# A graph network's attention stage: scores interleaved two source blocks at a time, and one mask product fewer

## What is computed

```python
q = x @ Wq + bq
k = x @ Wk + bk
v = x @ Wv + bv
logits = jnp.sum(q[dst] * k[src], axis=-1) * scale
m = jax.ops.segment_max(logits, dst, num_segments=n)
ex = jnp.exp(logits - m[dst])
denom = jax.ops.segment_sum(ex, dst, num_segments=n)
alpha = ex / denom[dst]
agg = jax.ops.segment_sum(alpha[:, None] * v[src], dst, num_segments=n)
out = agg + x @ Ws + bs
return jax.nn.elu(out)
```

## Time and profile before

| | |
|---|---|
| time, median of 3 runs | 849.43 us (847.42 to 849.62) |
| the profiled execution: its time, its span | 856.0 us, 854.2 us |
| PE busy, share of the span | 755.5 us, 88% |
| PE weight loads | 655.8 us, 77% |
| DVE | 740.0 us, 87% |
| ACT | 505.8 us, 59% |
| POOL | 263.3 us, 31% |
| mean granted TensorE clock | 0.983 of full speed |

### The profile page before, as it was taken

How to read it: one execution, slowest core, us unless ns; L and a number is a source line. 1 busy time by engine, 2 the same in 40 slices (tenths; PEclk the granted TensorE clock), 3 DMA queues, 4 the chain that set the end, 5 groups by cost and what they waited for, 6 DMA issues and landing times.

```text
span 854.2 us, 22930 instructions
## 1 busy us (share of the span) xinstructions
PE 755.5 (88%) x8801; PEld 655.8 (77%) x8848; DVE 740.0 (87%) x888; ACT 505.8 (59%) x1013; POOL 263.3 (31%) x205
## 2 busy tenths in 40 slices
PE   0258999999999999999999687899999999999996
PEld 0146777777777777777775466799999999999996
DVE  6776799999999999999994537899999999999982
ACT  4859766767677667676775251445456455445534
POOL 4634000000000000000000320556766766766766
PEclk9999999999999999999999798899999999999998
DMA  9821112313213123122131612203433433432400
GB/s 252 264 78 79 79 79 105 125 77 135 95 77 153 77 95 135 77 125 105 77 153 79 254 56 77 77 13 149 160 105 134 160 123 116 160 137 105 157 7 11
DMA packets 17661, 96.63 MB, mean 113 GB/s; under 512 B 2610, under 2 KB 8860, under 8 KB 11100
## 3 DMA queue, kind: packets, MB, share of 16 engines
q1 hardware_dynamic: 14572, 90.02, 27.8%
q0 software_dynamic: 3056, 6.17, 2.6%
HBM read 51.55 MB, written 44.63 MB: 113 GB/s over the span
## 4 chain that ended last, share of the span: by engine, by line
PE 70%; DVE 12%; issue 10%; ACT 5%; another core or an unknown queue 1%; DMA 1%; DVEq 1%; POOL 0%; POOLq 0%; ACTq 0%; PEldq 0%; PEld 0%
PE bank L1278 17%; PE bank L1288 16%; PE bank L1117 14%; PE bank L1107 5%; PE bank L1146 5%; DVE oh_key L901 5%; PE bank L1144 5%; DVE kT L838 3%; PE bank L1275 2%; PE bank L1241 2%; ACT kT L543 1%; PE bank L1246 1%; PE bank L1084 1%; DVE mx L1029 1%
## 5 line engine op out<-in xcount | busy, mean ns | idle before, releaser
L481 POOL TENSOR_TENSOR sm<-sm,mbc 128x896 f32<-128x896 f32 (+1 forms) x100 | 186.2, 1892 | 77.5 <-ACT mbc L703 77.5
L1117 PE MATMUL bank<-wsb,hvb 128*128 128x512 f32 (+1 forms) x350 | 165.2, 578 | 13.7 <-DVE kT L838 12.4
L1278 PE MATMUL bank<-qT,kT 128*128 (+1 forms) x1250 | 168.0, 279 | 6.9 <-issue 4.3
L1144 PE MATMUL bank<-oh_key,oh_lo 128*128 128x100 bf16 x1600 | 170.4, 208 | 1.9 <-ACT wst L607 1.9
L1146 PE MATMUL bank<-oh_key,oh_lo 128*128 128x50 bf16 x3200 | 170.8, 187 | 0.0
L1278 PEld LDWEIGHTS bank<-qT,kT 128*128 128x128 f32 x1250 | 163.8, 196 | 5.0 <-DVEq L178 1.2
L1146 PEld LDWEIGHTS bank<-oh_key,oh_lo 128*128 128x128 bf16 x3200 | 163.7, 97 | 1.1
L1144 PEld LDWEIGHTS bank<-oh_key,oh_lo 128*128 128x128 bf16 x1600 | 155.8, 97 | 7.7 <-issue 5.5
L589 ACT COPY wsb<-bank 128x512 f32<-128x512 f32 (+1 forms) x175 | 88.0, 552 | 106.4 <-PE bank L1107 106.4
L1288 PE MATMUL bank<-vals,sm 128*128 128x129 f32 x1250 | 148.5, 276 | 0.0
L1029 DVE TENSOR_REDUCE mx<-sm 128x128 f32<-128x3200 f32 x25 | 146.2, 5846 | 0.9
(11 more groups left out here) (123 smaller groups left out, 697.9 us busy)
## 6 DMA issues: line engine op xcount, KB each, us to landing
gt<-gst SPq DMA_DIRECT2D x25, 1600.0 KB, 5.6
gl_sb<-gt SPq DMA_DIRECT2D x25, 1600.0 KB, 6.7
records<-rec SPq DMA_DIRECT2D x1, 2015.0 KB
out<-res SPq DMA_DIRECT2D x24, 64.0 KB, 1.6
src_i<-in_src SPq DMA_DIRECT2D x1, 403.0 KB, 6.5
w_in<-in_edge_weight SPq DMA_DIRECT2D x1, 403.0 KB, 6.9
dst_i<-in_dst SPq DMA_DIRECT2D x1, 403.0 KB, 7.4
dstn_i<-in_dst_next SPq DMA_DIRECT2D x1, 403.0 KB, 7.3
```

Source lines behind the costliest of these rows:

```text
L481: pool.tensor_tensor(part, part, mbc[:, v % 2:v % 2 + 1, :].to_broadcast([P, n, P]), ALU.subtract).then_inc(sub_done, 1)
L1117: T.matmul(ps(6 + at)[:, 0:n], hvb[:, w, :], wsb[:, at, 0:n], start=True, stop=True).then_inc(l0_mm, 1)
L1144: T.matmul(cells, lo, oh_key[:, u, m, 0:2 * KEYS, i], start=True, stop=False, skip_group_check=True)
L1278: ins = T.matmul(score_bank(g)[:, j * P:(j + 1) * P], kT[:, (a + j) * P:(a + j + 1) * P], qT[:, bass.ds(t * P, P)], start=g < LIFT, stop=T ...
```

## The change

The groups become 6, 6, 6 and 8 blocks, which makes room for 26 (`NTP`): `sm` and `gl_sb` get a 26th block. It is set up once: its part of `gl_sb` to a large negative number by POOL, its place in the last group's PSUM bank to zero by DVE. `sm` is laid out in pairs of blocks, with the two values of one destination side by side (`twos`), so `mask` writes every other word of a pair's 256, the maximum reads two words side by side and then hops to the next pair, and the weights of a values product are 128 words 8 bytes apart. `LIFT` becomes 2: PE does no mask product for group 1, ACT's `absent` starts at group 2, and DVE lifts group 1 too.

```diff
-SG = [(0, 7), (7, 6), (13, 6), (19, 6)]
+SG = [(0, 6), (6, 6), (12, 6), (18, 8)]
+NTP = NT + 1
-LIFT = 1
+LIFT = 2
...
+        def twos(v, a, n):
+            return sm[:, v, a * P:(a + n) * P].rearrange("p (k d i) -> p k d i", d=P, i=2)
...
+            pool.memset(gl_sb[:, :, NT * P:NTP * P], -FLOOR).then_inc(pad_ready, 1)
...
-                    part = sm[:, v, a * P:(a + n) * P].rearrange("p (h d) -> p h d", d=P)
-                    pool.tensor_tensor(part, part, mbc[:, v % 2:v % 2 + 1, :].to_broadcast([P, n, P]),
-                                       ALU.subtract).then_inc(sub_done, 1)
+                    part = twos(v, a, n)
+                    top = mbc[:, v % 2, :].unsqueeze(1).unsqueeze(3).to_broadcast([P, n // 2, P, 2])
+                    pool.tensor_tensor(part, part, top, ALU.subtract).then_inc(sub_done, 1)
...
+            V.memset(score_bank(NSG - 1)[:, (NT - SG[-1][0]) * P:SG[-1][1] * P], 0.0).then_inc(pad_ready, 1)
...
-                V.tensor_tensor(sm[:, v, a * P:(a + n) * P], score_bank(g)[:, 0:n * P],
-                                gl_sb[:, v, a * P:(a + n) * P], ALU.add).then_inc(masked, 1)
+                V.tensor_tensor(twos(v, a, n).rearrange("p k d i -> p k i d"),
+                                score_bank(g)[:, 0:n * P].rearrange("p (k i d) -> p k i d", d=P, i=2),
+                                gl_sb[:, v, a * P:(a + n) * P].rearrange("p (k i d) -> p k i d", d=P, i=2),
+                                ALU.add).then_inc(masked, 1)
...
+                if live(t + 1):
+                    for g in range(1, LIFT):
+                        lift(t + 1, (v + 1) % RING, turn + (v + 1) // RING, g)
                 if now:
                     mask(t, v, 3)
                 if now:
                     dve.wait_ge(masked, 2 + (t + 1) * NSG)
-                    V.tensor_reduce(mx[:], sm[:, v, :].rearrange("p (h d) -> p d h", d=P), AX, ALU.max).then_inc(mx_ready, 1)
+                    V.tensor_reduce(mx[:], twos(v, 0, NTP).rearrange("p k d i -> p d k i"), AXY, ALU.max).then_inc(mx_ready, 1)
...
-                for h in range(a, a + n):
-                    ins = T.matmul(ps(4 + v % 2)[:, 0:D + 1], sm[:, v, h * P:(h + 1) * P], vals[:, h, :], start=h == 0,
+                for h in range(a, min(a + n, NT)):
+                    weights = twos(v, h - h % 2, 2).rearrange("p k d i -> p (k d) i")[:, :, h % 2]
+                    ins = T.matmul(ps(4 + v % 2)[:, 0:D + 1], weights, vals[:, h, :], start=h == 0,
```

More of the change, by code:

```diff
@@ L11 @@
 AX = mybir.AxisListType.X
+AXY = mybir.AxisListType.XY
 F32 = mybir.dt.float32
@@ L82 @@
 STEPS = NT + 3
-assert sum(n for _, n in SG) == NT and NSG % 2 == 0 and LOOP_TO < NT
+assert sum(n for _, n in SG) == NTP and all(n % 2 == 0 for _, n in SG) and NSG % 2 == 0 and LOOP_TO < NT
 TG = [(a, min(4, NT - a)) for a in range(0, NT, 4)]
@@ L287, in build_gnn @@
         res = sb(s4, "res", [P, 2, D])
-        sm = sb(s4, "sm", [P, RING, NT * P])
-        gl_sb = sb(s4, "gl_sb", [P, RING, NT * P])
+        sm = sb(s4, "sm", [P, RING, NTP * P])
+        gl_sb = sb(s4, "gl_sb", [P, RING, NTP * P])
         s4.close()
@@ L293, in build_gnn @@
         gl = [sem(f"gl{k}") for k in range(RING)]
-        absent_ready, lifted = sem("absent_ready"), sem("lifted")
+        absent_ready, lifted, pad_ready = sem("absent_ready"), sem("lifted"), sem("pad_ready")
         s_ready, masked, mx_ready, mt_ready, m_ready, dg_ready, mb_ready, mbc_ready = (
@@ L401, in load_g @@
                     sp.wait_ge(masked, 2 + (t - RING + 1) * NSG)
-                sp.dma_start(gl_sb[:, v, :], gt[bass.ds(tile, 1), :, :, :].rearrange("b p h n -> (b p) (h n)")).then_inc(gl[v], 16)
+                sp.dma_start(gl_sb[:, v, 0:NT * P], gt[bass.ds(tile, 1), :, :, :].rearrange("b p h n -> (b p) (h n)")).then_inc(gl[v], 16)
             for t in range(RING):
@@ L675, in mark_absent @@
                     act.wait_ge(s_ready, (t - 1) * NSG)
-                nc.scalar.activation(absent[:, v % 2, LIFTED:], gl_sb[:, v, LIFTED:], ACT.Relu, scale=-STEEP).then_inc(absent_ready, 1)
+                nc.scalar.activation(absent[:, v % 2, LIFTED:], gl_sb[:, v, LIFTED:NT * P], ACT.Relu, scale=-STEEP).then_inc(absent_ready, 1)
             root(0)
@@ L1028, in dve_step @@
                     dve.wait_ge(masked, 2 + (t + 1) * NSG)
-                    V.tensor_reduce(mx[:], sm[:, v, :].rearrange("p (h d) -> p d h", d=P), AX, ALU.max).then_inc(mx_ready, 1)
+                    V.tensor_reduce(mx[:], twos(v, 0, NTP).rearrange("p k d i -> p d k i"), AXY, ALU.max).then_inc(mx_ready, 1)
+            dve.wait_ge(pad_ready, 2)
             for g in range(LIFT):
@@ L1272, in scores @@
                 pe.wait_ge(masked, t * NSG + g + 1)
-                for b, e in ((0, 4), (4, n)):
+                for b, e in ((0, 4), (4, min(n, NT - a))):
                     if g >= LIFT:
```

## The result

The changed kernel takes 843.99 us, median of 12 runs, beside 849.27 us for the kernel before on the same chip: ratio 0.9941, 95% interval 0.9927 to 0.9954. That is 5.3 us faster, by the interval 3.9 to 6.2. I had forecast 837.5 (829 to 859), faster by 12, so the direction was right and the size less than half.

What follows compares the result with a forecast made beforehand. PE was taken to bound stage 4's step, with DVE close behind. Savings of 5.7 us over 21 steps, 5.5 at the start and 1.2 at the end, less 0.2 set-up, made 12.2: about 837.5 us, range 829 to 859.

Steps and rivals of the forecast that it cites:

- What bounds the kernel: Stage 4's step of 12.62 us: PE's own work 12.45 plus a 0.17 wait for mask 1; DVE occupied 12.02.
- either engine alone could gain almost nothing: Stage 4's step: work taken from only PE or only DVE leaves 12.62 us or little less.
- The maximum: DVE's maximum over blocks: 5.86 us falls to 3.5 with pairs; rival that pairs gain nothing, 867 us, chance 0.05.
- the masks' writes: DVE's masks writing every other word: no cost; rival of 0.78 ns an element, 867 us, chance 0.14.
- POOL: Subtraction on POOL: 7.45 us becomes 7.75, hidden; rival that POOL becomes the bound, 862 us, chance 0.05.
- PE's removed columns: PE's mask products: 640 columns fewer at 0.42 ns each, 0.267 us a step less.
- The weights 8 bytes apart: Values products' weight loads on PE: no cost taken; rival of 45 ns a load, 890 us or more, chance 0.03.
- the two ends that I kept, 0 and 45 ns: Cost range per strided weight load: none, from stage 2's line 1107, up to 45 ns, 2.3 us a step.
- DVE's occupied time: DVE in a stage 4 step: 12.02 us falls to 10.8, under PE's 12.35, idle 1.5 mostly ahead of mcol.
- The ends: Stage 4's first steps, where PE waits for the maximum: 5.5 us saved (4.0 to 7.3); its last: 1.2.
- Sums: Totals: 12.2 us saved, median 849.43 to about 837.5; chances given as faster 0.73, slower 0.22.

Runs made afterwards that it cites:

- e9: The changed kernel with DVE masking group 1 right behind group 0, ahead of the lift and mcol; ratio to the kernel before 0.9885, step 12.50 us.
- e10: The changed kernel with LIFT = 3 and DVE masking group 1 right behind group 0; ratio to the kernel before 0.9803, step 12.18 us.
- e4: The kernel before with only LIFT = 2, the second lift ahead of mask 3; ratio to the kernel before 0.9927, step 12.43 us.
- e1: The changed kernel with values products reading contiguous weights (blocks mixed up, same count and size); ratio to the kernel before 0.9866, step 12.36 us.
- e6: The changed kernel with LIFT = 3, group 2's mask product dropped too; ratio to the kernel before 0.9945, step 12.66 us.
- e5: The changed kernel run again with nothing edited, as control; ratio to the kernel before 0.9930, step 12.66 us.
- e3: The changed kernel with values products' weights 16 bytes apart in place of 8 (mixed up); ratio to the kernel before 1.1616, step 18.43 us.
- e11: e10 with the lift of the next tile's group 0 moved behind the reciprocal, ahead of mask 2; ratio to the kernel before 0.9814, step 12.18 us.
- e7: The changed kernel with LIFT = 4, no mask product on PE and no absent on ACT; ratio to the kernel before 1.0105, step 13.2 us.

## Why the prediction was right and wrong

- **What bounds the kernel**: right for PE, its own work and the wait for mask 1; e9 and e10 removed that wait from the changed kernel and got about what it measured (0.16 and 0.48 us). Wrong that either engine alone could gain almost nothing: e4 took work from PE alone, gave DVE more, and the step fell by 0.19.
- **The maximum, the masks' writes, POOL**: right. 3.62 us for a forecast 3.5, writes 8 bytes apart free, POOL faster than before (1654 ns for 768 elements, 1825 before), not slower.
- **PE's removed columns**: right, 0.27 us; e1's step of 12.36 us is the forecast 12.35.
- **The weights 8 bytes apart, "I take no cost"**: this is the step that failed. I set line 1107's strided loads beside line 1288's contiguous ones and read 0.113 against 0.112. But those belong to the turning products of stage 2, with one load each (625 for 25 x 25 blocks), and the values products have two (1250). Two different kinds of product stood side by side. Turning products with contiguous weights were in the trace as well, in stage 3:

```profile
487.70 0.58 PEld L1252 LDWEIGHTS bank<-ident,xn 128*128 128x128 f32 x5
```

  Five loads in 0.58 us, less one load's own 0.14, is 0.110 us from one to the next, so that the stride of line 1107 came with 3 ns and not 1, and with 0.19 us for a load of its own, not 0.14. No values product with strided weights was there. Why the two kinds differ in what a stride costs is not shown. Measured: 6 ns a load, 0.31 us a step, 25 x 0.31 = 7.7 us; the forecast gain of 12.2 less 7.7 is 4.5, and the table of stretches adds up to 4.6. Between the two ends that I kept, 0 and 45 ns, the whole gain of a step stood at 0.27 us, so the bounds should have said: over 5 ns a load the steady gain is gone.
- **DVE's occupied time**: 12.02 us before was too much by some 0.45, shown by e4. That made me expect the single edit `LIFT = 2` to lose, where it won as much as all of the change. For the changed kernel I forecast 10.8 us occupied and 1.5 idle, mostly ahead of `mcol`, and the trace shows 0.47 there: the lift behind the first mask, beside GpSimd's subtraction, is booked at 2.79 us and not at the 0.95 of the other. The slack lies inside it, and the forecast of the time did not fail by this: e6 put a third lift on DVE, and it still waited 0.47 us for PE.
- **The ends**: -4.5 and -1.0 us for forecast -5.5 and -1.2, near the low end of 4.0 to 7.3. The granted clock still fell to 0.50, the 1.2 GHz level, behind the first wait (522 to 524 us). In e5, the same kernel, the second turning comes 10.20 us behind the first, but the third 17.16 behind the second: the ends vary by half a microsecond from one execution to another.
- **Sums**: 849.43 - 12.2 is 837.2, not 837.5, and the chances as listed add up to 0.71 for faster and 0.24 for slower, not 0.73 and 0.22. Neither bears on the outcome.

## What to carry to other kernels

Price a strided operand from the same kind of instruction with the same number of loads, or call it open and work out at what price it eats the gain: here 5 ns did. When PE and another engine hand work to and fro within a step, removing work inside the stretch between the two hands brings nothing (e6) until the handshake is moved out of it (e10). And try each part of a change alone: `LIFT = 2` with the place of its lift (e4) gave what the whole did.

## What the runs showed of the hardware

- **Weight loads of the fp32 values products** follow each other at 0.112 us in a stream when contiguous, 0.118 with words 8 bytes apart, 0.23 with 16 (e1, the change, e3). The Trainium skill (SBUF — State Buffer, the note on "cachelines" in Door 1: The DMA port swizzle) asks for two accesses to a 16-byte line; the jump at 16 bytes agrees, the 6 ns at 8 bytes are not in it. That it also calls a step of 4 fp32 free, as the prediction repeats, these loads contradict: that step is the 16 bytes of e3, and the distance doubled. Why stage 2's loads 100 bytes apart show 0.113 stays open; contiguous turning products show 0.110, and no run tried one with another stride.
- **DVE's writes 8 bytes apart** are free (952 against 954 ns), though those 20 bytes apart cost 0.78 ns an element. The rule that only runs of at least two adjacent words keep the full rate (the Trainium skill, Vector Engine (DVE) Microarchitecture Reference, 5.2) doesn't hold for this step on the written side; for the maximum's pairs, read 1024 bytes apart at 1.04 ns an element, it does.
- **A lift beside GpSimd's subtraction waits for it.** Lifts take 951 ns in the median and 2794 at most in stage 4 of the changed kernel. The long one of the shown step starts at 708.28, GpSimd ends at 703.28 + 6.97 = 710.25, and the lift at 711.07, 0.82 later. In e11 it stands where GpSimd doesn't subtract, and all lifts have a mean of 947 ns. Masks, with one input in PSUM and one in SBUF, and the maximum run beside GpSimd's subtraction too and don't lengthen there (940 to 959 ns for 768 elements, 3619 to 3621). This agrees with the Trainium skill (SBUF — State Buffer, Who interferes with whom): an instruction of DVE with two inputs in SBUF contends with GpSimd's reads, and one with a single SBUF input doesn't. In e7 and e11 GpSimd's four take longer in turn (8.12 and 7.56 us in place of 6.97), where lifts start just ahead of them.
